# Attention kernel: the causal mask of the diagonal blocks moved from TensorE products to VectorE, and one order of uses for the spare PSUM bank

## The chip, the cores and the metric

The program runs on one NeuronCore of a Trainium2 chip. The metric is the device time of one execution in microseconds (us), as the median of several executions. A core has five engines, each with its own in-order instruction stream: TensorE (PE, with its weight loads shown apart as PEld), VectorE (DVE), ScalarE (ACT), GpSimd (POOL) and SyncE (SP, which here only issues DMAs). They are ordered among each other by semaphores alone. PE writes to eight PSUM banks of 128 partitions by 512 fp32 values.

## The reference

The program computes two transformer-like layers. The change is in the attention of the first one, with 8 batches of 512 tokens, 16 heads of size 8, and two score maps for each head:

```
s1 = jnp.einsum('bhqd,bhkd->bhqk', q1, k1) * scale
s2 = jnp.einsum('bhqd,bhkd->bhqk', q2, k2) * scale
a1 = jax.nn.softmax(jnp.where(causal, s1, neg_inf), axis=-1)
a2 = jax.nn.softmax(jnp.where(causal, s2, neg_inf), axis=-1)
comb = a1 - lam[None, :, None, None] * a2
out = jnp.einsum('bhqk,bhkv->bhqv', comb, v)
```

A layer norm over each head's 16 outputs, a product with `Wo` and a gated residual follow, and then a feed-forward layer, a state-space scan and a mixture of experts, which the change leaves alone.

## The kernel before

**Tiling.** The attention works in rounds, one for each batch (r), and each round in 8 slots (g), one for each group of two heads, so four score maps. The tokens are four blocks of 128. Each map's scores are computed twice. The first time (tile `p1b`, query rows on the partitions, product line L616) serves only to find each row's maximum: DVE reduces a bank over the keys into `bmax` (L853), and at the slot's end all partial maxima into `qneg` (L864). POOL splits the negated maximum into two bf16 parts (`nsp`), PE turns them (`turn_neg`, L731 into the spare bank `auxb`), ACT copies them out (L582) and SP's DMA puts them into the query stack `qs` as extra rows. Two slots later the scores are computed again, transposed and with the maximum already subtracted (tile `p2b`, L668), and ACT takes the exponential into `pT` (L558). POOL zeroes what lies above the diagonal in `pT` (L519). One slot later the products with the values go to `ob` (L682), and one more later the result is copied (`o_sb`, L564), turned (L723) and copied into `oT` (L573).

**Units.** A group's lower triangles are packed into ten banks, called units, handled in five pairs t = 0 to 4: pairs 0 and 2 (units 0, 1, 4, 5) hold the four diagonal blocks of a map each, the others only whole blocks below the diagonal. `p1b` and `p2b` are rings of three banks each, so the first product of a pair waits until DVE has read the first unit of the pair before (semaphore `first_read`, in `bank_free`), and the second product in the same way for ACT's exponential.

**The mask.** Scores above the diagonal must not count in the maximum. Before the four diagonal products of a bank, PE multiplies an identity with the table `causal` (-3e38 above the diagonal, four times side by side, bf16) and lets the scores add onto it: the mask product, L620, four a slot.

**The spare bank.** `auxb` is used in turn for everything else that PE must produce: the turned result, the turned maxima, the transposed input of the next batch (L776, copied to `hT` by ACT at L602), its four projections (`project`, L743; ACT copies the high part at L587, DVE makes the remainder `res` at L858, ACT its middle part at L568, POOL the rest at L540, and SP stores the three parts), its four value products (L770, copied at L598), and for the batch before the turned normalized result (L752) and the product with `Wo` (L763). Each kind has its own pair of semaphores.

**Who does what in a slot.** While a round computes batch r, it prepares batch r+1 (`prep`: transposes in g=0, projections in g=1 to 4, values in g=2 to 5) and finishes batch r-1 (`post`: reciprocals in g=4, POOL's weighted sums in g=4 and 5, DVE's normalization between the units of g=5 and 6, L825 to L839, the output product at the end of g=7, read by DVE at L867). The order is written out by hand in each engine's `slot`. Slot -1 is a prologue that only prepares batch 0.

Of the kernel before, what the change touches and what calls it, by code (L numbers as in the profile page):

```python
# [13 lines left out]
BF16 = mybir.dt.bfloat16  # L14
# [7 lines left out]
P = 128  # L22
# [299 lines left out]
MAPS = 4  # L322
# [10 lines left out]
DIAGONAL, EDGE, MIDDLE = "diagonal", "edge", "middle"  # L333
FIRST = ((DIAGONAL, 0), (EDGE, 0), (DIAGONAL, 1), (EDGE, 1), (MIDDLE, None))
# [14 lines left out]
def lagged(r, g, n):  # L349

    return (r, g - n) if g >= n else (r - 1, g - n + GROUPS)

# [7 lines left out]
def attention(nc, d, k):  # L360
# [3 lines left out]
    with ExitStack() as ctx:  # L364
# [6 lines left out]
        def sem(name):  # L371
# [3 lines left out]
        causal = sb("causal", [P, TILES, P], BF16)  # L375
# [25 lines left out]
        xn_ready, xnT_done, hT_ready, qk_done, hi_ready, res_ready, mid_ready, split_ready, v_done, v_ready = (  # L401
            sem(n) for n in ("xn_ready", "xnT_done", "hT_ready", "qk_done", "hi_ready", "res_ready", "mid_ready",
                             "split_ready", "v_done", "v_ready"))
# [3 lines left out]
        first_unit, first_read, second_unit, exp_done, masked, vs_ready, av_done, o_read, oT_done, oT_read = (  # L407
            sem(n) for n in ("first_unit", "first_read", "second_unit", "exp_done", "masked", "vs_ready", "av_done", "o_read",
                             "oT_done", "oT_read"))
        qneg_ready, nsp_high, nsp_ready, neg_psum, neg_ready = (  # L410
            sem(n) for n in ("qneg_ready", "nsp_high", "nsp_ready", "neg_psum", "neg_ready"))
        rc_ready, og_ready, merged_ready, mT_done, mT_ready, wo_done, gated_ready, post_done = (
            sem(n) for n in ("rc_ready", "og_ready", "merged_ready", "mT_done", "mT_ready", "wo_done", "gated_ready", "post_done"))
# [6 lines left out]
                   oT_done: 2, oT_read: 4, neg_psum: 2, nsp_ready: 2, xnT_done: 1, res_ready: 1, split_ready: 1, v_done: 1, v_ready: 1,  # L420
                   qk_saved[0]: 16, qk_saved[1]: 16, og_ready: 2, merged_ready: 1, mT_done: 1, wo_done: 1, gated_ready: 3, neg_ready: 1, hT_ready: 1}
# [27 lines left out]
        def _(sp):  # L449
# [13 lines left out]
            def slot(r, g, on, prep, post):  # L463
                if on(1):
                    rn, gn = lagged(r, g, 1)
                    sp.wait_ge(neg_ready, rn * GROUPS + gn + 2)
# [78 lines left out]
        def _(act):  # L545
            act.wait_ge(slots_set, 1)

            def slot(r, g, on, prep, post):
# [44 lines left out]
                if prep and 2 <= g < 6:  # L593
                    c, V = g - 2, b * TILES + g - 2
                    act.wait_ge(v_done, V + 2)
                    if c == 0:
                        act.wait_ge(vs_ready, b * GROUPS + 1)
# [10 lines left out]
        def _(pe):  # L608
# [64 lines left out]
            def product(G, a, c):  # L673
# [10 lines left out]
                if c == TILES - 1:  # L684
                    mm.then_inc(av_done, 1)
# [1305 lines left out]
```

## Time and profile before

| | |
|---|---|
| median of 3 runs | 1892.64 us (1891.42 to 1895.62) |
| the profiled execution | 1895.24 us, of it 1893.5 between its first and last instruction |
| busy: PE, DVE, ACT, POOL | 1383.6, 1330.0, 1033.1, 949.4 us |
| attention | about 75 to 835 us of the span |
| mean granted clock of TensorE | 0.839 of full speed |

The busy times are sums over an engine's instructions in the profiled execution. An instruction's row names its line, the tile written and the tiles read, the shape, and, in square brackets, the idle time of its engine ahead of it with what ended that.

### The profile page before, as it was taken

What the parts mean: (1) busy time and instruction counts of PE and PEld (TensorE: products, weight loads), DVE (VectorE), ACT (ScalarE), POOL (GpSimd) and SP (SyncE); (2) the same over time, 40 slices, a digit from 0 to 9 for tenths busy, and PEclk for the clock granted to TensorE, in tenths of its full rate; (3) what the DMA queues carried; (4) which work ended last, traced back from release to release, by engine and by line L of the source; (5) the groups of instructions that cost most, each with busy time, mean ns of one, the idle gap of its engine ahead of it and who ended that gap; (6) DMA issues with size and microseconds to landing.
All of it is one profiled execution on the core that took longest, in us unless ns stands there. A gap on an engine that the chain in (4) does not pass through costs nothing. (4 is left out here: it accounts for less than half of the span.)

```text
span 1893.5 us, 29677 instructions
## 1 busy us (share of the span) xinstructions
PE 1383.6 (73%) x8526; PEld 602.3 (32%) x8589; DVE 1330.0 (70%) x2162; ACT 1033.1 (55%) x1605; POOL 949.4 (50%) x850
## 2 busy tenths in 40 slices
PE   3588888888888888754674465556655788898898
PEld 2133333333333333322342122122212344444343
DVE  3667767676767677836776499999987666566654
ACT  1166666666666566643652444334422677767776
POOL 2032424242424242433882566666772567676677
PEclk7579888888889899876887677777877899999999
DMA  3221313131313131100003354544553766666675
GB/s 96 92 89 48 102 34 100 34 100 34 100 34 100 34 100 39 32 1 0 1 0 92 101 179 162 173 168 165 182 184 115 168 161 170 158 174 170 168 184 137
DMA packets 114314, 197.96 MB, mean 105 GB/s; under 512 B 16300, under 2 KB 49736, under 8 KB 114248
## 3 DMA queue, kind: packets, MB, share of 16 engines
q1 hardware_dynamic: 112808, 195.08, 35.9%
q10 hardware_dynamic: 1440, 2.10, 0.4%
q8 instruction: 30, 0.49, 0.1%
q14 instruction: 36, 0.29, 0.1%
HBM read 167.76 MB, written 28.84 MB: 104 GB/s over the span
## 5 line engine op out<-in xcount | busy, mean ns | idle before, releaser
L853 DVE TENSOR_REDUCE bmax<-p1b 128x4 f32<-128x512 f32 x640 | 414.1, 687 | 183.5 <-PE p1b L616 176.8
L558 ACT ACTIVATE pT<-p2b 128x512 f32<-128x512 f32 x640 | 349.4, 604 | 122.2 <-PE p2b L668 121.1
L1701 POOL TENSOR_TENSOR hid_l<-e_hid,hid_h 128x1024 f16<-128x1024 f32 (+1 forms) x136 | 281.3, 2077 | 134.3 <-ACT hid_h L1843 133.8
L1339 PE MATMUL yb<-ch,ident 128*128 128x512 f32 x256 | 175.8, 825 | 130.3 <-POOL ch L1272 86.9
L1959 DVE TENSOR_TENSOR e_hid<-ub,share 128x1024 f32<-128x1024 f32 x128 | 156.1, 1224 | 152.6 <-ACT ub L1856 131.9
L510 POOL CAST nsp<-qneg 128x16 bf16<-128x16 f32 x64 | 12.7, 198 | 482.7 <-DVE qneg L864 482.7
L682 PE MATMUL ob<-pT,vs 128*32 128x512 f32 (+3 forms) x2048 | 202.4, 482 | 1.3 <-POOL pT L519 1.3
L668 PE MATMUL p2b<-qs,ks 50*128 50x512 bf16 (+3 forms) x1024 | 137.4, 328 | 51.5 <-ACT pT L558 49.8
L1856 ACT ACTIVATE ub<-ub 128x1024 f32<-128x1024 f32 x128 | 129.2, 1009 | 83.3 <-PE ub L1757 81.6
L616 PE MATMUL p1b<-ks,qs 48*128 48x128 bf16 (+2 forms) x1792 | 139.3, 264 | 37.2 <-DVE bmax L853 37.1
L1843 ACT ACTIVATE hid_h<-e_hid 128x1024 f16<-128x1024 f32 (+1 forms) x136 | 139.2, 1024 | 26.8 <-DVE e_hid L1959 26.7
L519 POOL TENSOR_SCALAR_AFFINE_SELECT pT<-pT 128x1280 f32<-128x1280 f32 (+2 forms) x192 | 145.4, 790 | 11.6 <-ACT pT L558 11.6
L1439 ACT ACTIVATE dA<-dt,nA 128x511 f32<-128x511 f32 (+1 forms) x128 | 85.2, 712 | 98.3 <-DVE hs L1529 45.0
L1272 POOL TENSOR_TENSOR ch<-hs,crow 128x1024 f32<-128x1024 f32 x32 | 75.3, 2352 | 119.5 <-DVE hs L1529 93.8
L1339 PEld LDWEIGHTS yb<-ch,ident 128*128 128x128 f32 x256 | 59.8, 253 | 234.8 <-POOL ch L1272 110.1
L1755 PE MATMUL ub<-e_hTh,w_high 128*128 (+1 forms) x256 | 100.9, 394 | 22.2 <-DVE e_hid L1959 22.2
L620 PE MATMUL p1b<-causal,identb 128*128 128x512 bf16 x193 | 91.3, 473 | 35.0 <-DVE bmax L853 22.2
L1529 DVE TENSOR_TENSOR_SCAN hsb<-dA,dBx 128x1024 f32<-128x1024 f32 x32 | 108.8, 3400 | 7.6 <-ACT dA L1439 4.7
L668 PEld LDWEIGHTS p2b<-qs,ks 50*128 50x128 bf16 x1024 | 35.0, 96 | 227.5 <-ACT pT L558 137.7
L1755 PE MATMUL e_yb<-hid_h,w_high 128*128 128x512 f16 x264 | 101.7, 385 | 4.7 <-POOL hid_l L1701 4.0
L1756 PE MATMUL e_yb<-hid_l,w_high 128*128 128x512 f16 x264 | 101.5, 384 | 0.0
L1757 PE MATMUL e_yb<-hid_h,w_low 128*128 128x512 f16 x264 | 101.1, 383 | 0.0
(258 smaller groups left out, 2652.5 us busy)
## 6 DMA issues: line engine op xcount, KB each, us to landing
share<-shares SPq DMA_DIRECT2D x256, 256.0 KB, 4.2
brow<-bc_rows SPq DMA_DIRECT2D x64, 512.0 KB, 4.8
crow<-bc_rows SPq DMA_DIRECT2D x64, 512.0 KB, 4.0
q_stacks<-parts SPq DMA_DIRECT2D x96, 128.0 KB
k_stacks<-parts SPq DMA_DIRECT2D x96, 128.0 KB
qs<-q_stacks SPq DMA_DIRECT2D x128, 96.0 KB, 2.2
ks<-k_stacks SPq DMA_DIRECT2D x128, 96.0 KB, 2.3
qs<-nparts SPq DMA_DIRECT2D x128, 4.0 KB
```

Of the source, the lines that this page charges most:

```text
L519: pool.affine_select(out=block_ap, in_=block_ap, compare_op=ALU.is_ge, fill=0.0, base=0, pattern=[[0, n], [1, P]], channel_multiplier=-1). ...
L558: act.activation(pT[:, g2 % 2, stored(w), :], p2b[bank_of(g2, w)][:, :], ACT.Exp, scale=SCALE).then_inc(exp_done, 1)
L616: return pe.matmul(bank[:, at * P:(at + blocks[1] - blocks[0]) * P], qs[rows, slot, head, c * P:(c + 1) * P], ks[rows, slot, head, blocks[ ...
L668: mm = pe.matmul(p2b[bank_of(g, 2 * t + j)][:, at:at + S - c * P], ks[rows, slot, head, c * P:(c + 1) * P], qs[rows, slot, head, c * P:S], ...
L682: mm = pe.matmul(ob[32 * m:32 * m + 32, c * P:S], vs[:, a, c, m // 2, :], pT[:, a, u, at:at + n], start=(c == 0), stop=(c == TILES - 1), s ...
L853: dve.tensor_reduce(to, bank, AX, ALU.max).then_inc(first_read, 1)
L1339: mm = pe.matmul(yb[:, :], k.ident[:, :], ch[:, m % 4, j, :], start=False, stop=(m == PAIRS - 1 and j == 1), skip_group_check=True)
L1701: pool.tensor_tensor(flat(hid_l[:, place(p), 0:n, :]), flat(hid[:, place(p), 0:n, :]), flat(hid_h[:, place(p), 0:n, :]), ALU.subtract).the ...
L1755: pe.matmul(to, w[0], high, start=start, stop=False, skip_group_check=True)
L1843: act.activation(flat(hid_h[:, place(p), 0:n, :]), flat(hid[:, place(p), 0:n, :]), ACT.Copy).then_inc(hid_rounded, 1)
L1856: act.activation(u, u, ACT.Silu, scale=1.0 / W_SCALE).then_inc(silu_ready, 1)
L1959: dve.tensor_tensor(h, u, flat(share[:, p % SHARES, :, :]), ALU.mult).then_inc(hid_ready, 1)
```

## The change

Three things change. The first is the mask: the mask products go, the first diagonal product of a bank starts the bank itself, and DVE replaces the one reduction of a diagonal bank by four instructions, one for each 128 columns, that add the table `causal` (now one block of 128x128 fp32) to the scores, write the sum to a tile `spare` that nobody reads, and take its maximum into `bmax`. The second is the numbering: all uses of `auxb` get a number in one fixed order (`aux_of`), counted by two semaphores, `aux_done` for PE and `aux_read` for the reader, and every use waits until the use before it is read. The third is a table of places: the value products of a slot come at t=4, for g=3 to 6, ahead of the last products into `ob`; the transposes of `xn` likewise in g=0; `hT` is copied behind ACT's last exponentials of g=0; the middle copy of a projection moves from t=0 to t=1 on ACT; and `res` from ahead of unit 9 to ahead of unit 7 on DVE.

```
+AUX = {"turn_o": 1, "turn_neg": 2, "project": 3, "value": 4, "turn_x": 4, "turn_m0": 3, "turn_m1": 4, "wo": 5}
+AV_AT = (2, 3, 4, 4)
+O_COPY_AT, OT_AT, NEG_COPY_AT, HIGH_AT, MID_AT, HT_AT, V_COPY_AT, MT_AT = 0, 1, 2, 3, 1, 4, 4, (3, 4)
+RES_AT = 6
...
+def aux_of(g):
+
+    kinds = ["turn_o", "turn_neg"]
+    if g == 0:
+        kinds.append("turn_x")
+    if 1 <= g < 5:
+        kinds.append("project")
+    if 3 <= g < 7:
+        kinds.append("value")
+    if g == GROUPS - 1:
+        kinds += ["turn_m0", "turn_m1", "wo"]
+    return sorted(kinds, key=AUX.get)
...
-        causal = sb("causal", [P, TILES, P], BF16)
+        causal = sb("causal", [P, P])
+        spare = sb("spare", [P, MAPS, TILES, P], BF16)
...
-            def mask(bank):
-                pe.matmul(bank[:, :], k.identb[:, :], causal[:, :, :].rearrange("p c t -> p (c t)"), start=True, stop=False, skip_group_check=True)
...
                 if kind == DIAGONAL:
-                    mask(bank[1])
                     for c in range(TILES):
                         for j in range(2):
-                            mm = score(bank[j], c, slot, head, j, c, (c, c + 1), False)
+                            mm = score(bank[j], c, slot, head, j, c, (c, c + 1), c == 0)
...
+                def aux_free(kind):
+
+                    n = aux_use(r, g, kind)
+                    if not isinstance(r, int) or n > 0:
+                        pe.wait_ge(aux_read, n)
...
                         if kind == DIAGONAL:
-                            to = bmax[:, g % 2, 2 * j + head, 8:8 + 3 * BLOCK_STEP + 1:BLOCK_STEP]
+                            dve.sem_inc(passed, 1)
+                            for c in range(TILES):
+                                at_c = 8 + c * BLOCK_STEP
+                                ins = dve.tensor_tensor_reduce(spare[:, u // 4 * 2 + j, c, :], bank[:, c, :], causal[:, :], 1.0, NEG, ALU.add, ALU.max,
+                                                               bmax[:, g % 2, 2 * j + head, at_c:at_c + 1])
+                            ins.then_inc(first_read, 1)
+                            to = None
...
-                    if prep and u == 8 and 1 <= g < 5:
+                    if prep and u == RES_AT and 1 <= g < 5:
```

In the built program, DVE's stream for one plain slot begins before with its first three rows, and continues with the reductions of whole blocks:

```order
L853 TENSOR_REDUCE bmax<-p1b 128x4 x8
L853 TENSOR_REDUCE bmax<-p1b 128x2x2
L858 TENSOR_TENSOR res<-auxb,parts 128x512
L853 TENSOR_REDUCE bmax<-p1b 128x2x2
L864 TENSOR_REDUCE qneg<-bmax 128x16
```

Now one diagonal unit and the rows around it read as follows; an `ISA` row with `bmax 128x1` is the read of the accumulator that the instruction above it left:

```order
L868 ISA spare,bmax<-p1b,causal 128x128
L868 ISA bmax 128x1
L868 ISA spare,bmax<-p1b,causal 128x128
L868 ISA bmax 128x1
L878 TENSOR_REDUCE bmax<-p1b 128x4 x2
```

One reduction has become four pairs of instructions, 32 rows a slot where four stood.

On PE, in a slot with a projection and a value product (g=3) and up to the next slot's first products, before:

```order
L682 MATMUL ob<-pT,vs 32x384 x4
L743 MATMUL auxb<-hT,wqk 128x512
L668 MATMUL p2b<-qs,ks 128x256 x4
L616 MATMUL p1b<-ks,qs 128x256 x4
L682 MATMUL ob<-pT,vs 32x256 x4
L682 MATMUL ob<-pT,vs 32x128 x4
L620 MATMUL p1b<-causal,identb 128x512
L620 MATMUL p1b<-causal,identb 128x512
L616 MATMUL p1b<-ks,qs 128x128 x8
L770 MATMUL auxb<-wv,hT 128x256
```

And in the changed program at the same place (L749 is the projection, L755 the value product, L699 the products into `ob`):

```order
L749 MATMUL auxb<-hT,wqk 128x512
L699 MATMUL ob<-pT,vs 32x384 x4
L684 MATMUL p2b<-qs,ks 128x256 x4
L641 MATMUL p1b<-ks,qs 128x256 x4
L755 MATMUL auxb<-wv,hT 128x256
L699 MATMUL ob<-pT,vs 32x256 x4
L699 MATMUL ob<-pT,vs 32x128 x4
L641 MATMUL p1b<-ks,qs 128x128 x8
```

The masks are gone, and the value product has moved from behind the next slot's first products to ahead of the last products into `ob`; the projection stands one place earlier.

On ACT, the start of slot g=2 before (L558 is the exponential, L564 the copy of `ob`, L568 the middle copy, L573 the copy into `oT`):

```order
L558 ACTIVATE pT<-p2b 128x512
L558 ACTIVATE pT<-p2b 128x512
L564 ACTIVATE o_sb<-ob 128x512
L568 ACTIVATE parts<-res 128x512
L558 ACTIVATE pT<-p2b 128x512
L558 ACTIVATE pT<-p2b 128x512
L573 ACTIVATE oT<-auxb 128x4x68
```

And now (the same kinds at L583, L589, L593 and L599):

```order
L583 ACTIVATE pT<-p2b 128x512
L583 ACTIVATE pT<-p2b 128x512
L589 ACTIVATE o_sb<-ob 128x512
L583 ACTIVATE pT<-p2b 128x512
L583 ACTIVATE pT<-p2b 128x512
L593 ACTIVATE parts<-res 128x512
L599 ACTIVATE oT<-auxb 128x4x68
```

The middle copy has moved behind the second pair of exponentials and stands directly ahead of the copy into `oT`.

## Rows read from the trace of the kernel before

**Rows 1.** the page: busy us of each engine, share of the span, instructions

```profile
PE 1383.6 (73%) x8526; PEld 602.3 (32%) x8589; DVE 1330.0 (70%) x2162; ACT 1033.1 (55%) x1605; POOL 949.4 (50%) x850
```

**Rows 2.** `qneg` instructions: ns min/median/max, first and last start

```profile
L864 DVE TENSOR_REDUCE qneg<-bmax x64: 236/240/246, 84.5 to 812.2; 128x16 f32<-128x80 f32 x64
```

**Rows 3.** windows, slots g=0 to 7: length, busy (instructions), granted clock, DMA share, GB/s

```profile
440.11:455.81 15.70, 12.57 (x109) 5.97 (x111) 9.13 (x18) 7.39 (x14) 3.01 (x6) 0.78 0.08 25
455.81:468.68 12.87, 10.92 (x103) 4.56 (x102) 7.29 (x13) 8.00 (x16) 2.99 (x6) 0.87 0.14 41
468.68:478.38 9.70, 8.52 (x89) 3.62 (x90) 7.10 (x13) 7.33 (x15) 4.12 (x7) 1.00 0.17 48
478.38:488.98 10.60, 9.05 (x93) 3.75 (x92) 7.19 (x12) 7.66 (x16) 4.12 (x7) 1.00 0.37 110
488.98:500.17 11.19, 9.12 (x93) 3.69 (x92) 9.10 (x15) 7.96 (x16) 8.00 (x9) 1.00 0.32 98
500.17:512.85 12.68, 9.10 (x91) 3.74 (x90) 10.17 (x15) 7.16 (x15) 6.45 (x8) 0.92 0.43 133
512.85:526.11 13.26, 11.13 (x92) 4.05 (x94) 11.60 (x26) 7.92 (x16) 2.99 (x6) 0.69 0.23 70
526.11:535.65 9.54, 8.95 (x84) 3.80 (x85) 6.50 (x11) 6.55 (x13) 2.99 (x6) 0.82 0.04 9
sum 95.54, PE 79.36 PEld 33.18 DVE 68.08 ACT 59.96 POOL 34.66; mean PE 9.92 PEld 4.15 DVE 8.51 ACT 7.50 POOL 4.33
```

**Rows 4.** the same for one slot of the last round, without preparation

```profile
748.60:757.15 8.55, 7.19 (x95) 3.10 (x91) 6.70 (x12) 6.58 (x13) 2.99 (x6) 1.00 0.17 51
```

**Rows 5.** waits in 200 to 700 us: total, times, longest

```profile
DVE bmax L853 <- PE p1b L616: 117.4, 121, 2.1
```

**Rows 6.** timeline of that slot: start, duration, engine; [idle before <-releaser]

```profile
751.31 0.38 PE L620 MATMUL p1b<-causal,identb 128*128 128x512 bf16 x1
...
751.62 0.39 PE L668 MATMUL p2b<-qs,ks 50*128 50x512 bf16 x2
...
756.42 0.16 PEld L620 LDWEIGHTS p1b<-causal,identb 128*128 128x128 bf16 x2 [0.20 <-issue]
...
756.97 0.40 PE L616 MATMUL p1b<-ks,qs 48*128 48x128 bf16 x8
```

**Rows 7.** timeline of DVE, three places without waits; below, groups: busy, mean ns

```profile
61.54 5.50 DVE L884 BATCH_NORM_STATS2 bn<-x_tok 128x6 f32<-128x128 f32 x28
...
491.20 2.47 DVE L853 TENSOR_REDUCE bmax<-p1b 128x4 f32<-128x512 f32 x4
...
1708.85 0.08 DVE L1922 MATCH_VALUE_LOAD rest<-top,biased 128x8 f32 x1
1708.92 0.21 DVE L1922 MATCH_REPLACE8 rest<-top,biased 128x64 f32<-128x64 f32 x1
...
L853 DVE TENSOR_REDUCE bmax<-p1b 128x4 f32<-128x512 f32 x640 | 414.1, 687 | 183.5 <-PE p1b L616 176.8
...
L884 DVE BATCH_NORM_STATS2 bn<-x_tok 128x6 f32<-128x128 f32 x64 | 12.7, 276 | 0.5 <-PEq L364 0.5
...
L887 DVE BATCH_NORM_AGGREGATE stats<-bn 128x2 f32<-128x6 f32 x64 | 4.7, 151 | 0.1
...
L867 DVE TENSOR_TENSOR gated<-auxb,gate_a 128x512 f32<-128x512 f32 x8 | 5.5, 692 | 26.0 <-PE auxb L763 26.0
```

**Rows 8.** timeline of all engines, in g=1 and at half clock in g=0

```profile
456.94 0.78 ACT L602 ACTIVATE hT<-auxb,mod 128x512 f32<-128x512 f32 x1 [1.60 <-PE auxb L776]
...
542.04 0.61 PE L616 MATMUL p1b<-ks,qs 48*128 48x384 bf16 x4 [2.23 <-DVE bmax L853]
...
543.48 0.63 PE L620 MATMUL p1b<-causal,identb 128*128 128x512 bf16 x1
```

**Rows 9.** timeline of ACT in g=2, the middle copy of a projection

```profile
470.07 0.64 ACT L568 ACTIVATE parts<-res 128x512 bf16<-128x512 f32 x1
```

**Rows 10.** timeline of POOL in the prologue, the table

```profile
29.75 0.65 POOL L492 TENSOR_SCALAR_AFFINE_SELECT causal<-causal 128x512 bf16<-128x512 bf16 x1
```

More of the change, by code:

```diff
@@ L351, in lagged, with aux_use @@
     return (r, g - n) if g >= n else (r - 1, g - n + GROUPS)
+def aux_of(g):
[9 more added lines that the diff above has]
+    return sorted(kinds, key=AUX.get)
+AUX_PLACE = {use: n for n, use in enumerate((g, kind) for g in range(GROUPS) for kind in aux_of(g))}
+AUX_USES = len(AUX_PLACE)
+def aux_use(r, g, kind):
+    return (r + 1) * AUX_USES + AUX_PLACE[g, kind]
 def stored(w):
@@ new lines, in side @@
+                    if kind == "value":
+                        if not prep:
+                            return skip(kind)
+                        c = g - 3
+                        aux_free(kind)
+                        mm = pe.matmul(auxb[:, 0:H * VD], hT[:, c * P:(c + 1) * P], k.wv[:, :], start=True, stop=True)
+                    if kind in ("turn_m0", "turn_m1"):
+                        if not post:
+                            return skip(kind)
+                        c = int(kind[-1])
@@ new lines, in side @@
+                    mm.then_inc(aux_done, 1)
+                for t in range(PAIRS + 1):
+                    if t == PAIRS:
+                        if g + 1 < GROUPS and on(0) or g + 1 == GROUPS and prep:
+                            rl, gl = (r, g + 1) if g + 1 < GROUPS else (r + 1, 0)
+                            pe.wait_ge(stack_loaded[gl % RING], (use(rl, gl) + 1) * LOADS)
+                            first_pair(rl, gl, 0)
+                    else:
+                        if on(2):
+                            r2, g2 = lagged(r, g, 2)
+                            if t == 0:
+                                pe.wait_ge(neg_loaded[g2 % RING], (use(r2, g2) + 1) * NEG_LOADS)
+                            second_pair(r2, g2, t)
+                        if on(0) and t:
+                            first_pair(r, g, t)
+                    for kind in aux_of(g):
+                        if AUX[kind] == t:
+                            side(kind)
+                    if on(3):
+                        r3, g3 = lagged(r, g, 3)
+                        for n in range(len(CHUNKS)):
+                            if AV_AT[n] == t:
+                                product(r3 * GROUPS + g3, g3 % 2, n)
```

254 lines of the change are left out of this document (105 added, 149 removed).

## Prediction, made before the changed kernel ran

> **What bounds the kernel now.** The page's busy line names no saturated engine: PE 73%, VectorE (DVE) 70% of the span [rows 1]. So I read the windows of one middle round of the attention, cut at the starts of the reduction into `qneg`, which ends each slot on DVE. The 64 slots start their last work between 84.5 and 812.2 us [rows 2], 63 steps of 11.55 us on average. One round takes 95.54 us, with PE busy 79.36, DVE 68.08, ACT 59.96 [rows 3]. No engine is full; the slots are of two kinds. In g=1 to 3 and 7 PE sets the pace: PE has 8.5 to 10.9 us of work and DVE idles 2.6 to 5.6 us of the slot. In g=4 to 6 DVE does the normalization of the last batch between its bank reductions and has 9.1 to 11.6 us of work in 11.2 to 13.3 us. A slot without preparation, of the last round, takes 8.55 us with PE at 7.19 and DVE at 6.70 [rows 4]. The whole change therefore moves work from PE to DVE where the two are 10% apart: PE leads in most slots, and after the change DVE will.
>
> What holds PE in such a slot is its ring with ACT (the second product of a pair waits for the exponential of the pair before) and its ring with DVE (three banks): in 500 us of the middle rounds DVE waits for first products 117.4 us in 121 places [rows 5], which is most of its idle time.
>
> **What the change removes, on PE.** Four mask products a slot, 32 a round. From the starts in one slot the first costs 0.31 us (751.31 to 751.62), the second as much, the two ahead of the next slot 0.55 (their weight load at 756.42 to the product behind them at 756.97) [rows 6]: 1.17 us a slot at full clock. Walking the 8.55 us slot without them, all else as it stands, PE's own path would be 7.4 us.
>
> **What it adds, on DVE.** Four of ten reductions a slot go; each becomes four times a 128-column add-and-maximum from PSUM and a read of the accumulator, 16 pairs a slot. Neither operation is in the trace. Nearest rows for the cadence when nothing is waited for: 28 statistics of 128 columns took 5.50 us, so (5.50-0.276)/27 = 0.193 us from start to start, 128 columns at 1.04 ns and 0.060 fixed; four reductions of 512 columns from PSUM took 2.47 us, (2.47-0.687)/3 = 0.594, again 0.061 fixed; and a tiny instruction that loads state for the next one (8 columns) holds its successor for 0.07 us [rows 7]. A pair is then 0.193 + 0.062 = 0.255. Bounds: below, nothing can beat the 128 columns plus one fixed part, 0.193. Above, if each of the two ran alone to its end, the duration of the statistics, 0.276, plus that of a 12-column aggregate, 0.151: 0.427 [rows 7]. I take 0.256, because the loader pair is the nearest kind (two instructions that share engine state) and it isn't held. That the second operand is an fp32 table shouldn't matter: the product of a PSUM bank with an fp32 gate takes 0.692 for 512 columns, as the reduction does (0.687) [rows 7].
>
> The Trainium skill speaks to this twice. "VectorE: DVE Perf Modes", section on two Vector instructions with no wait between them, says that an operation with accumulator output is two instructions, each judged on its own, and held only when start quadrants change; here all start at partition 0. It would give the 0.256 that I take. "Vector Engine (DVE) Microarchitecture Reference", section 5.2, puts the fixed part at about 75 ns; an estimate by it is a pair of 0.284 and a sum of about 1899 us, no gain. The rows here (60 and 61 ns) are below its figure.
>
> So DVE's own work in a plain slot is 16 x 0.256 + 6 x 0.594 + 0.3 (`qneg`, and the gap to the first unit) + 4 x 0.05 (a wait at each unit) = 8.2 us, against PE's 7.4. Break-even with the 8.55 of now is a pair of 0.278.
>
> **The walk through the rings.** Unit 0 of a diagonal pair now frees its bank after 1.1 us instead of 0.69, so PE's next first product starts 0.4 later. But it has then unit 1 (another 1.05) for 0.43 us of product and latency, so DVE doesn't starve. That is why I let DVE run nearly without gaps in plain slots.
>
> **The numbered spare bank and the moved copies.** These edits change waits. (1) The copy into `hT` and the transposes of `xn` come before the next slot's first exponentials. Now ACT waits 1.60 us for the transposes and copies for 0.78 before it can start them [rows 8], and PE's next first product and DVE stand behind those: with DVE in the lead, this goes from g=1. (2) The subtraction `res` moves from ahead of unit 9 to ahead of unit 7. It needs ACT's high copy of the projection, which comes some 0.75 us later than DVE gets there: a new DVE stall of 0.75 in g=1 to 3. (3) The middle copy moves on ACT from before the exponentials of t=1 to behind them, ahead of the copy into `oT`, 0.64 long [rows 9]. PE's `turn_neg` waits for `oT`; with its masks gone PE arrives about 0.6 earlier than now, so it stands there: about 0.3 of g=2 and 3 reaches DVE. Behind it in PE's queue are the products into `ob`, which nobody needs soon. (4) The value product now stands ahead of the last products into `ob` and of the next slot's first product, and waits for `res`; 0.1 more in g=3. Where DVE has its own extra work (g=4 to 6) these are hidden.
>
> Slot by slot, now and after (us):
> g=0: 15.70, 14.0 (1.0 less of waiting for the output product, since the two masks in front of it go and DVE arrives 0.5 later; 1.1 for two masks at half clock; 0.4 more until the first bank is free)
> g=1: 12.87, 9.8 (8.2 + 0.6 `res` + 0.75 stall + 0.2; item 1)
> g=2: 9.70, 10.0
> g=3: 10.60, 10.1
> g=4: 11.19, 11.7 (8.2 + 2.0 reciprocal and gate + 0.6 + 0.9)
> g=5: 12.68, 12.8 (8.2 + 3.7 of three 1024-column steps, + 0.9 until POOL's sum is there)
> g=6: 13.26, 14.0 (8.2 + 5.8)
> g=7: 9.54, 9.3 (PE: 7.4 + two sets of transposes, partly at half clock)
> Sum 95.5 to 91.7.
>
> The granted clock takes some of it back. It stands at 1.00 in g=2 to 4 and at 0.69 in g=6, where PE waits for DVE [rows 3]; behind a wait of 2.23 us for DVE a mask product takes 0.63 instead of 0.38 us [rows 6, 8], the lower of the two levels, 1.2 GHz for 2.4. With DVE in the lead PE waits more. I add 0.8: a round of 92.5, so 3.0 saved.
>
> Sum: six middle rounds x 3.0 = 18; the first 2.5, the last 1; the prologue 1.5, of it some 0.8 for a table a quarter as wide, which POOL clears and fills (the fill alone 0.65 now [rows 10]), which DVE waits for at the start. Together 23. The profiled execution took 1895.24, the median of the runs is 2.6 lower: 1895.2 - 23 - 2.6 = 1870 us.
>
> **Rivals.** What a measurement can tell from no change is about 0.2%, 4 us.
> *The read of the accumulator waits for the sum* (slower; it ends on the other side). Then the pair is 0.276 + 0.062 = 0.338, 0.082 more; x 16 x 64 = 84 us more, 1954. For: it reads what the instruction before it makes. Against: the loader pair isn't held. From 0.28 on it decides. Fully serial, 0.427, it would be 175 more, 2045.
> *A larger fixed part.* The accumulating form may start 0.014 us later each than the instructions of [rows 7] do; with 28 ns more in a pair, 1024 pairs cost 29 us, 1899. For: these two instructions are in no row. Against: three kinds of instruction there agree within 0.01. (This is the second page's case.)
> *The clock.* PE at half clock needs some 12 us for a plain slot (7.4 by 0.63/0.38, [rows 6, 8]), more than DVE's 8.2. If g=1, 2, 3 and 7 spend half their time so, each gains 1.5: +6 a round, 1918. For: PE's busy share falls from 0.84 [rows 4] to about 0.7 in plain slots. Against: while PE is slow it is busy all the time, and in g=2 and 3 it keeps the projection and 80% share.
> *The new stalls eat the gain*: items 2 to 4 at twice my size, 3 a round, 24 us: 1889 to 1895, no change. For: they stand in four slots of eight; against: each was walked from rows.
>
> **How the numbers follow.** My forecast 0.52 (1845 to 1888); pair held, partly or fully, 0.18 (of it 0.10 above 1958); larger fixed part 0.06; clock 0.14; stalls eat it 0.10. Faster: 0.50 of the first, 0.04 of the last two, 0.54; same 0.07; slower 0.39. The range leaves out 0.10 above and some 0.06 below: 1848 to 1958.
>
> **What would show it.** The durations and starts of the four add-and-maximum instructions of a unit: 1.0 us from first to fifth start if I am right, 1.35 or 1.7 if held. The `qneg` starts 92 to 93 us apart from round to round; DVE busy over 80 of them, PE under 72. The wait of DVE for the high copy where `res` stands, and ACT's 1.60 us wait for the transposes gone. A granted clock in g=2 and 3 clearly under 1 would make the clock rival right. I'd be wrong above all through the pair: 0.01 us in it is 10 us of the kernel.

## The result and the profile after

The changed kernel took 1898.89 us (median of 7 runs, 1897.21 to 1902.93), the kernel before, on the same chip, 1892.28 us (7 runs, 1883.02 to 1895.62). The ratio is 1.0043, 95% interval 1.0023 to 1.0063: slower, by about 0.4%, where 1870 us and faster was forecast. The time lies inside the stated range (1848 to 1958), on the wrong side of the kernel before. A few executions of the kernel before, of e9 and of e14 further down ran far slower at a lower clock; the ratios leave them out, and e14's trace isn't read, since its profiled execution was one of them.

The busy line of the page, beside [rows 1], and VectorE's two new kinds of row (count, total us, mean ns, idle before them):

```profile
PE 1359.2 (72%) x8333; PEld 592.1 (31%) x8333; DVE 1389.7 (73%) x3954; ACT 1031.5 (54%) x1605; POOL 950.2 (50%) x850
...
L868 DVE CUSTOM_DVE_ANT_0 spare<-p1b,causal 128x128 bf16<-128x128 f32 x1024 | 228.0, 286 | 30.2 <-PE p1b L641 21.2 <-DVE vsum L849 1.9 <-DVE msum L843 1.9
L868 DVE DVE_READ_ACCUMULATOR2_ANT bmax<- 128x1 f32 x1024 | 84.5, 83 | 0.0
```

Work moved from PE to DVE as intended. The windows between the starts of `qneg` in a middle round, g=0 to 7 (it is the round behind that of [rows 3]; the second to sixth middle rounds are alike within 0.2 us, in either kernel):

```profile
540.48:557.63 17.15, 11.27 (x109) 5.85 (x108) 10.07 (x45) 7.23 (x15) 3.00 (x6) 0.80 0.08 24
557.63:568.98 11.35, 9.75 (x100) 3.73 (x96) 8.17 (x40) 7.28 (x15) 2.98 (x6) 0.85 0.16 46
568.98:579.65 10.67, 9.05 (x88) 3.39 (x86) 8.17 (x41) 7.50 (x15) 4.12 (x7) 0.84 0.19 57
579.65:590.25 10.60, 9.47 (x90) 3.82 (x88) 8.16 (x40) 7.88 (x16) 4.12 (x7) 0.84 0.37 110
590.25:602.89 12.64, 9.82 (x92) 3.79 (x88) 10.02 (x42) 8.04 (x16) 7.98 (x9) 0.86 0.32 95
602.89:616.02 13.13, 8.87 (x92) 3.57 (x90) 11.24 (x42) 8.13 (x17) 6.44 (x8) 0.87 0.39 119
616.02:629.66 13.64, 10.39 (x88) 3.86 (x86) 12.45 (x54) 6.99 (x15) 2.99 (x6) 0.63 0.21 61
629.66:639.49 9.83, 8.54 (x82) 3.63 (x78) 7.67 (x39) 6.97 (x14) 2.99 (x6) 0.83 0.04 11
sum 99.01, PE 77.15 PEld 31.64 DVE 75.95 ACT 60.02 POOL 34.62; mean PE 9.64 PEld 3.96 DVE 9.49 ACT 7.50 POOL 4.33
```

The round takes 99.01 us for 95.54. Three of eight slots are clearly longer: g=0 by 1.5, g=2 by 1.0 and g=4 by 1.5; g=1 gained 1.5. The granted clock in g=2 to 4, at 1.00 before, is 0.84 to 0.86. PE is busy longer in g=3 than before (9.47 for 9.05) although four products went. In a slot without preparation, of the last round, the gain is there, 7.67 us for the 8.55 of [rows 4]:

```profile
759.05:766.72 7.67, 6.57 (x86) 2.79 (x84) 7.47 (x40) 6.38 (x13) 2.99 (x6) 1.00 0.18 55
```

DVE's timeline at the start of a round, with PE's next product, and DVE's waits from 200 to 700 us (total, times, longest):

```profile
547.38 1.15 DVE L920 TENSOR_SCALAR xn<-x_tok,stats,rstd 128x128 f32 x4 [2.77 <-issue]
548.48 0.29 DVE L868 CUSTOM_DVE_ANT_0 spare<-p1b,causal 128x128 bf16<-128x128 f32 x1
548.69 0.08 DVE L868 DVE_READ_ACCUMULATOR2_ANT bmax<- 128x1 f32 x1
548.69 0.29 DVE L868 CUSTOM_DVE_ANT_0 spare<-p1b,causal 128x128 bf16<-128x128 f32 x1
...
549.47 0.61 PE L641 MATMUL p1b<-ks,qs 48*128 48x384 bf16 x4 [5.19 <-DVE bmax L868]
```

```profile
DVE res L883 <- ACT parts L613: 23.6, 21, 1.2
DVE xn L920 <- issue: 13.2, 5, 2.8
```

A pair of instructions costs 0.21 us (548.48 to 548.69). But DVE now stands for 2.77 us ahead of the first instruction of a round, waiting for nothing that the profile shows, five times; the five are the five jumps back of the loop over the middle rounds. PE waits 5.19 us behind it. DVE also waits about 1.1 us at each `res`.

### The profile page after: what moved, and what is told of

Same layout as the page of the kernel before. It is cut to its first block and busy times, and to the rows that moved or that the text cites. A ratio compares the mean times of both kernels' runs of the same rounds, so it can differ in the third digit from the quotient of the medians.

```text
span 1897.1 us, 31496 instructions
## 1 busy us (share of the span) xinstructions
PE 1359.2 (72%) x8333; PEld 592.1 (31%) x8333; DVE 1389.7 (73%) x3954; ACT 1031.5 (54%) x1605; POOL 950.2 (50%) x850
## 5 line engine op out<-in xcount | busy, mean ns | idle before, releaser
L583 ACT ACTIVATE pT<-p2b 128x512 f32<-128x512 f32 x640 | 349.9, 605 | 189.9 <-PE p2b L684 189.1
L878 DVE TENSOR_REDUCE bmax<-p1b 128x4 f32<-128x512 f32 x384 | 248.2, 685 | 56.9 <-PE p1b L641 52.4
L1364 PE MATMUL yb<-ch,ident 128*128 128x512 f32 x256 | 180.8, 845 | 125.9 <-POOL ch L1297 87.5
L868 DVE CUSTOM_DVE_ANT_0 spare<-p1b,causal 128x128 bf16<-128x128 f32 x1024 | 228.0, 286 | 30.2 <-PE p1b L641 21.2
L699 PE MATMUL ob<-pT,vs 128*32 128x512 f32 (+3 forms) x2048 | 231.6, 543 | 2.0 <-POOL pT L544 1.3
L641 PE MATMUL p1b<-ks,qs 48*128 48x128 bf16 (+2 forms) x1792 | 147.0, 274 | 116.1 <-DVE bmax L868 70.0
L684 PE MATMUL p2b<-qs,ks 50*128 50x512 bf16 (+3 forms) x1024 | 142.9, 340 | 45.7 <-ACT pT L583 45.2
L544 POOL TENSOR_SCALAR_AFFINE_SELECT pT<-pT 128x1280 f32<-128x1280 f32 (+2 forms) x192 | 145.3, 790 | 10.1 <-ACT pT L583 10.1
L641 PEld LDWEIGHTS p1b<-ks,qs 48*128 48x128 bf16 x1792 | 69.8, 106 | 182.4 <-DVE bmax L868 90.0
```

The costliest lines, as they stand in the source:

```text
L544: pool.affine_select(out=block_ap, in_=block_ap, compare_op=ALU.is_ge, fill=0.0, base=0, pattern=[[0, n], [1, P]], channel_multiplier=-1). ...
L583: act.activation(pT[:, g2 % 2, stored(w), :], p2b[bank_of(g2, w)][:, :], ACT.Exp, scale=SCALE).then_inc(exp_done, 1)
L641: return pe.matmul(bank[:, at * P:(at + blocks[1] - blocks[0]) * P], qs[rows, slot, head, c * P:(c + 1) * P], ks[rows, slot, head, blocks[ ...
L684: mm = pe.matmul(p2b[bank_of(g, 2 * t + j)][:, at:at + S - c * P], ks[rows, slot, head, c * P:(c + 1) * P], qs[rows, slot, head, c * P:S], ...
L699: mm = pe.matmul(ob[32 * m:32 * m + 32, q0:q1], vs[:, a, c, m // 2, :], pT[:, a, u, at:at + q1 - q0], start=(n == 0), stop=(n == len(CHUNK ...
L868: ins = dve.tensor_tensor_reduce(spare[:, u // 4 * 2 + j, c, :], bank[:, c, :], causal[:, :], 1.0, NEG, ALU.add, ALU.max, bmax[:, g % 2, 2 ...
```

## Experiments

All figures in one place first. "Last" is the start of the last `qneg` in the profiled execution, where the attention's maxima end. After it the programs took another 1073 to 1087 us, whatever the mask, so it tells more about the attention than the total does. The attention lost 11.4 us by it, more than the total did; what follows the attention differs by up to 13 us between the profiled executions. Kernels of different groups ran on different chips; the ratio is to the kernel before on the same chip.

| kernel | median us | ratio, 95% interval | last, us |
|---|---|---|---|
| before | 1892.28 | 1 | 812.2 |
| changed | 1898.89 | 1.0043, 1.0023 to 1.0063 | 823.6 |
| e1 mask alone | 1907.47 | 1.0102, 1.0064 to 1.0140 | 823.1 |
| e2 numbering and places alone | 1875.09 | 0.9909, 0.9878 to 0.9941 | 792.9 |
| e3 changed, rounds written out | 1881.37 | 0.9949, 0.9926 to 0.9971 | 797.1 |
| e4 before, rounds written out | 1866.89 | 0.9879, 0.9852 to 0.9905 | 788.6 |
| e5 changed, loop shifted | 1889.36 | 1.0008, 0.9984 to 1.0032 | 810.8 |
| e6 changed, idle mask products | 1916.47 | 1.0146, 1.0112 to 1.0181 | 840.9 |
| e7 half the masks on DVE | 1895.15 | 1.0027, 1.0006 to 1.0048 | 812.1 |
| e8 e2, rounds written out | 1864.90 | 0.9870, 0.9836 to 0.9905 | 785.6 |
| e9 e2, longer DVE loop | 1889.17 | 0.9983, 0.9967 to 0.9999 | 812.1 |
| e10 e2, transposes of `xn` later | 1873.53 | 0.9913, 0.9880 to 0.9945 | 806.5 |
| e11 changed, `res` later | 1884.94 | 0.9971, 0.9953 to 0.9990 | 807.4 |
| e12 e8, masks on DVE at the ends | 1866.47 | 0.9864, 0.9834 to 0.9895 | 778.0 |
| e13 changed, written out, `res` later | 1859.83 | 0.9841, 0.9809 to 0.9873 | 773.1 |
| e14 e13, half the masks on PE | 1889.29 | 0.9954, 0.9923 to 0.9985 | not read |
| e15 e8, `res` later | 1864.25 | 0.9840, 0.9816 to 0.9865 | 782.6 |
| e16 e15, some masks on DVE | 1878.41 | 0.9937, 0.9915 to 0.9960 | 793.5 |

### Which part of the change lost

**e1** is the kernel before with the mask of the change alone; **e2** the changed kernel with its numbering and places, and the mask products and single reductions of before:

```
e2, against the changed kernel:
+                    mask(bank[1])
-                            mm = score(bank[j], c, slot, head, j, c, (c, c + 1), c == 0)
+                            mm = score(bank[j], c, slot, head, j, c, (c, c + 1), False)
...
+                            to = bmax[:, g % 2, 2 * j + head, 8:8 + 3 * BLOCK_STEP + 1:BLOCK_STEP]
```

> The kernel before with only the mask moved to VectorE (the sixteen add-and-maximum pairs a slot; DVE's loop over the middle rounds grows as in the changed kernel); numbering and places of the kernel before. Theory 'fetch' (the loss is the 2.8 us wait of DVE at the loop's back edge, which comes from the longer loop, and PE's half clock behind it): the wait is here too, and the time is 1890 to 1903, near the changed kernel. Theory 'places' (the early remainder, the late middle copy and the moved products lose it): no 1.2 us waits of the remainder for ACT's high copy, and the time is 1870 to 1885. If both hold, half and half: about 1885 with the back-edge wait in the rows. Theory 'clock' (DVE leads, PE idles and falls to half clock whatever the order): 1890 to 1905, clocks under 0.9 in g=1 to 4 without the wait being the reason.

> The changed kernel's numbering and places, with the mask products and single reductions of the kernel before. Theory 'places': slower than the kernel before by 8 to 25 us (1900 to 1917), with a wait of the remainder for ACT's high copy of up to 1 us in g=1 to 4. Theory 'fetch': DVE's loop is short again, no wait at the back edge, and the time is within 6 us of the kernel before (1886 to 1898), faster if the earlier hT copy counts.

Both missed their forecasts: e1 is slower than any theory had it, e2 faster. The parts pull in opposite ways. The numbering with its places gains 0.9%, the mask by itself loses 1.0%; between e2 and the changed kernel lie 1.3%. "Places" is refuted as the cause by itself: the stall that I had forecast at `res` stands in e2 (DVE waits for the high copy 21 times there too) and e2 is the faster one. e1 has the wait at the jump back (13.1 us in five).

### The wait at the jump back

In **e3**, **e4** and **e8** the middle rounds of the changed kernel, of the one before and of e2 are written out:

```
-            with eng.Fori(1, B - 1) as r:
+            for r in range(1, B - 1):
```

> The changed kernel with its six middle rounds written out one after the other on every engine, in place of the hardware loop: the same instructions in the same order, no branch back. Theory 'fetch': the 2.77 us wait ahead of the first normalization instruction of each round goes, PE's 5 us wait behind it shrinks, and the kernel is 15 to 30 us faster than the changed one: 1870 to 1884. Theory 'places' or 'clock': the slots g=0 and g=1 hardly change, 1892 to 1900. Instruction loading itself costs something everywhere: 1900 or more, with waits for nothing in the middle of rounds.

> The kernel before with its middle rounds written out in the same way: what the unrolling does by itself. No DVE wait at the back edge stands in its trace, so by theory 'fetch' it stays within 4 us of the kernel before (1888 to 1896); if unrolling helps or hurts by itself it does so here as well, and the difference to the run before it is what the changed kernel's longer loop costs.

> Numbering and places of the change, masks on PE (as in the second experiment), middle rounds written out on every engine. The second experiment showed PE waiting 2.6 us for no other engine at its own back edge. Unrolled it should lose that: six rounds of 2.3 to 3.9 us, 1852 to 1862. If the gain of unrolling in the kernel before (23 us) came from something else, for example from a lucky order of the clock, this one stays at 1870 to 1878.

The wait is gone from e3, with 17 us by the medians. But writing out also gained 10 us over e2 (e8) and 23 over the kernel before (e4, against its forecast), and in neither e2 nor the kernel before does DVE have such a wait. In e2 it is PE that waits, at the same jump; the second row is e2's branch on PE's sequencer, the third the same branch in the kernel before (ns min/median/max of six passes, of which the last doesn't jump):

```profile
PE p2b L692 <- issue: 11.3, 5, 2.6
```

```profile
L467 PEldq COMPARE_BRANCH  x6: 82/3807/4244, 245.8 to 710.0; - x6
```

```profile
L443 PEldq COMPARE_BRANCH  x6: 76/208/239, 249.8 to 727.7; - x6
```

So an engine waits at the jump for itself. PE's wait stands in e2, e6, e9 and e10, and neither in the kernel before nor in the changed one, although the loops of e2 and of the kernel before hardly differ on PE (891 and 886 instructions in the trace beside the products); why is open. In the kernel before no engine waits: on each the next instruction starts within 0.4 us of the branch. What e4 gained, 3.4 us a round, lies in g=0 and g=1, 15.70 and 12.87 us at clocks of 0.78 and 0.87 in [rows 3]:

```profile
427.55:441.48 13.93, 11.50 (x113) 5.68 (x113) 9.01 (x18) 7.37 (x14) 2.98 (x6) 0.88 0.11 30
441.48:452.66 11.18, 9.54 (x104) 3.97 (x98) 7.29 (x12) 7.78 (x16) 2.98 (x6) 1.00 0.17 49
```

DVE's normalization `xn` starts there 4.1 us after the slot's start, for 4.6 with the loop. That this half microsecond is what raised the clock is not shown. So e3 alone doesn't tell how much of its 17 us is the wait. In the changed kernel DVE's wait of 2.77 us comes on top of PE's path (it starts after DVE has read the output product, which PE makes early in the slot). Written out, the changed kernel is still 16 us slower than e2 written out (e3 against e8, on different chips; 0.8% by the ratios).

**e5** shifts the loop in DVE's stream, **e9** lengthens DVE's loop in e2 by 100 instructions that lie in waits, **e7** puts only units 0 and 1 on DVE. The counts in the texts below (244, 344, 356, 468) leave out some register and semaphore instructions: between two jumps of DVE the trace holds 248 in the kernel before, 250 in e2, 355 in e9, 378 in e7 and 505 in the changed kernel.

```
e5:
+            for i in range(80):
+                dve.memset(pad[:, i:i + 1], 0.0)
             dve.wait_ge(slots_set, SET)
e9:
+                    lengthen(60, 100)
                     dve.wait_ge(aux_done, aux_use(r, g, "wo") + 1)
...
+                        lengthen(15 * j, 15 * j + 15)
                         dve.wait_ge(hi_ready, J + 1)
e7, DVE:
+                        if kind == DIAGONAL and u >= 4:
+                            to = bmax[:, g % 2, 2 * j + head, 8:8 + 3 * BLOCK_STEP + 1:BLOCK_STEP]
```

> The changed kernel with 80 one-column memsets added to VectorE's stream in the prologue, inside its 9.2 us wait for POOL's tables, so that they cost nothing by themselves; all they do is shift where the loop's 468 instructions lie in the stream: from 451 to 919 in the changed kernel to 531 to 999 here. Theory 'where the loop lies' (instructions are held in aligned blocks of 256, two at a time; the loop of the changed kernel touches three, that of the kernel before, 227 to 469, two, and this one two again): the 2.77 us wait ahead of the first normalization instruction of each middle round is gone, g=0 goes from 17.1 to about 14.3, the kernel 12 to 20 us faster than the changed one: 1879 to 1887. Theory 'loop length' (it is the 468 instructions themselves or the branch, wherever they lie): nothing changes, 1896 to 1901, and the wait stays.

> The second experiment's kernel (numbering and places of the change, masks on PE) with 100 one-column memsets a round added on VectorE where it waits for others anyway: 40 ahead of its wait for the output product, 15 ahead of each wait for ACT's high copy. One took 28 ns in the padded kernel, so 2.8 us a round, all of it inside waits. DVE's loop grows from 244 to 344 instructions, and its work otherwise stays. Theory 'loop length': a wait of 2.5 to 3.4 us for nothing appears ahead of the first normalization instruction of each middle round, as in the half-mask kernel with its 356, and g=0 grows by up to 2.8 us where PE's own wait at the back edge doesn't cover it: 1878 to 1892 against 1875. Theory 'kind of instruction' (the accumulating instructions or their second form cause the wait, not their number): no such wait, 1872 to 1879.

> Half of the change's mask: units 0 and 1 are masked on VectorE as in the changed kernel, units 4 and 5 by mask products on PE as before; numbering and places are the changed kernel's. DVE's loop has 356 instructions, at 339 to 695, in two aligned blocks of 256. Theory 'where the loop lies': no 2.8 us wait of DVE at the back edge. Each mask moved costs DVE 0.25 us and saves PE 0.29; with half of them PE keeps 0.6 us more work a slot than in the changed kernel. If wait and clock are what the change lost, this is faster than both the kernel before and the changed one: 1868 to 1880. If moving any mask costs in proportion, it lies half way between the masks on PE (1875) and the changed kernel (1899): 1887.

DVE's waits at the loop's first instruction, e5, e9 and e7:

```profile
DVE xn L923 <- issue: 16.4, 5, 3.4
```

```profile
DVE xn L933 <- issue: 13.0, 5, 2.7
```

```profile
DVE xn L940 <- issue: 13.2, 5, 2.7
```

e9 settles that it isn't the kind of instruction: no mask is on DVE, g=1 to 3 are as long as in e2, and the wait is there, with 14 us of time (g=0 takes 17.8 to 18.5 us for 13.3 to 16.7). In e5, 80 instructions further on, the wait is longer, not gone. But this doesn't refute "where the loop lies": a loop of 505 instructions fits into two blocks of 256 at 8 of 256 places alone, so the shift could hardly have done what that theory asked of it. Length and place aren't told apart by these runs. e5's time fell between its two forecasts, and not for a shorter wait: g=1 ran at 1.00 in every middle round, 9.8 us for 11.35.

```profile
451.60:461.38 9.78, 8.09 (x99) 3.41 (x96) 8.18 (x41) 7.28 (x15) 2.98 (x6) 1.00 0.20 54
```

The Trainium skill's page "Runtime: NRT & Kernel Launch", section "Instruction fetch mechanics", has a rule of this kind: a jump back to code outside the two blocks of 256 instructions that are held makes the engine wait for a fetch. The waits agree with it in kind. That its two blocks give the border seen no run shows: 248 and 250 instructions went without a wait, 355, 378 and 505 did not, and where a block begins in the stream no trace tells.

### PE's clock

**e6** is the changed kernel with PE's old mask products on top, over a table of zeros:

```
+                pe.matmul(bank[:, :], k.identb[:, :], flat[:, :, :].rearrange("p c t -> p (c t)"), start=True, stop=False, skip_group_check=True)
```

> The changed kernel, its masks on VectorE, but PE also does the four mask products a slot of the kernel before, with a table of zeros, so that they change no value: PE has its old work, DVE its new. Theory 'clock' (without the mask products PE's share of work falls, its clock drops to 0.84 to 0.87 in g=1 to 4, and that is what makes these slots 10.6 to 11.4 us long): the clock goes back to 1.00 in g=1 to 3, the slots come to 10.9, 10.1, 10.2 and 12.0, and the kernel is 5 to 12 us faster than the changed one although it does more: 1887 to 1894. Theory 'DVE sets the pace' (the slots are long for the sum of DVE's own work and its waits): the same 1896 to 1901. Theory 'PE sets the pace': slower by up to 1.2 us a slot in the plain slots and g=1 to 3, 1910 to 1930.

Windows of g=1 to 3, of e6 and then of e2:

```profile
471.53:482.26 10.73, 9.56 (x105) 3.73 (x102) 8.08 (x40) 7.42 (x15) 2.98 (x6) 1.00 0.16 51
482.26:492.22 9.96, 8.72 (x98) 3.44 (x92) 8.08 (x40) 7.50 (x15) 4.12 (x7) 1.00 0.17 46
492.22:502.26 10.04, 8.80 (x90) 3.40 (x84) 8.09 (x40) 7.88 (x16) 4.14 (x7) 1.00 0.40 119
```

```profile
445.14:455.87 10.73, 9.39 (x104) 3.74 (x102) 7.29 (x13) 7.41 (x15) 2.98 (x6) 1.00 0.18 49
455.87:465.83 9.96, 8.66 (x98) 3.48 (x92) 7.23 (x13) 7.49 (x15) 4.12 (x7) 1.00 0.16 45
465.83:475.87 10.04, 8.74 (x90) 3.44 (x84) 7.23 (x12) 7.87 (x16) 4.14 (x7) 1.00 0.40 118
```

With more to do PE ran g=1 to 3 at 1.00, and these slots came out 0.6 to 0.7 us shorter than in the changed kernel, to the hundredth those of e2: DVE's 0.8 us of extra work is hidden there. The clock theory holds for them, but not for the whole: g=0 grew to 18.7 us and g=4 stayed at 0.87, so that e6 is the slowest of all. In g=0 of e6 PE has also a wait at the jump, which it doesn't have in the changed kernel; how much of the growth that is isn't shown:

```profile
PE p2b L695 <- issue: 11.8, 5, 2.7
```

The plain comparison is within one kernel. In e3 the same slot g=1 of two rounds:

```profile
445.24:454.56 9.32, 7.55 (x88) 3.13 (x86) 8.13 (x41) 6.97 (x14) 2.99 (x6) 1.00 0.18 49
```

```profile
537.83:549.08 11.25, 9.40 (x96) 3.77 (x92) 8.18 (x41) 7.10 (x15) 2.99 (x6) 0.85 0.14 40
```

The same slot of the program, 1.9 us apart, a little of it because eight products fell on the other side of its edge. At 0.85 part of the slot ran at 1.2 GHz. e13, below, has the pair with equal counts.

### The places

**e10** is e2 with `"turn_x": 5`, **e11** the changed kernel with `RES_AT = 8`, **e15** that change in e8.

> The second experiment's kernel with one number changed: the transposes of the next input stand behind the first products of g=1 on PE, as in the kernel before, instead of ahead of them. If the prediction's first item is what the numbering gained (12.9 to 10.7 us in g=1), g=0 and g=1 together give back 1 to 2.2 us a round, 7 to 14 us: 1882 to 1889. If the gain of g=1 came from the clock or from the rest of the table, within 3 us of 1875.

> The changed kernel with the remainder ahead of unit 9 again in place of unit 7. In the changed kernel DVE waits 1.0 to 1.2 us there for ACT's high copy in g=1 to 4. Theory 'that stall is paid' (prediction's item 2): the wait goes, and each of the four slots loses 0.5 to 1.0 us: 12 to 24 us faster, 1875 to 1887. Theory 'the slots follow PE at its lower clock': DVE waits the same time for PE's products elsewhere, the slots stay within 0.3 us, and the kernel within 5 us of 1899; a slot changes only where its clock does.

> e8 (rounds written out, numbering and places of the change, masks on PE) with the remainder ahead of unit 9 again. DVE waits 1.0 us for the high copy in g=1 to 4 in e8, but PE leads there: nothing should come of it, 1862 to 1868. If the wait is paid even where PE leads, 0.3 to 0.5 us in three slots of six rounds: 1855 to 1860.

e10's time is e2's, as its second forecast had it: in the medians the earlier transposes are worth nothing that shows. In the trace g=1 takes 11.33 us at full clock in one round for 10.73 in e2, and 12.8 to 12.9 at 0.87 in most others: at equal clock the slot is 0.6 us longer. The profiled execution took 1883.55 us, 10 above the kernel's median, so its windows stand for an unlucky case.

e11 is 0.7% faster than the changed kernel, as its first forecast had it: the wait for the high copy was paid, where DVE leads. Its g=2 in two successive rounds shows which way:

```profile
462.70:473.32 10.62, 9.07 (x86) 3.49 (x86) 8.17 (x40) 7.68 (x17) 4.10 (x7) 0.84 0.21 61
```

```profile
557.32:566.74 9.42, 7.80 (x86) 3.09 (x86) 8.18 (x40) 7.49 (x17) 4.11 (x7) 1.00 0.18 52
```

At 0.84 nothing changed (10.62 for 10.67). The gain is in slots that now reach 1.00, g=1 and 2 in three of the six middle rounds (g=3 in two of them) and g=4 in the other three; at 1.00 the wait itself is worth 0.2 (e5 had 9.64 there in one round, `res` early). In e15, where PE leads, g=2 and 3 are 0.35 us shorter each, g=4 and 5 are 0.5 and 0.6 longer, and the time is e8's, as forecast.

### Masks where they pay

**e12** is e8 with the masks on DVE in the first round and in g=1 to 3 of the last. **e13** is the changed kernel with both of DVE's waits removed (rounds written out, `RES_AT = 8`), **e14** the same with units 4 and 5 masked on PE. **e16** is e15 with masks on DVE as in e12 and, in the middle rounds, in pair 0 of g=1 to 4 and 7:

```
+def on_vector(r, g, t):
+
+    return r == 0 or r == B - 1 and 1 <= g < 4 or t == 0 and (r < B - 1) and g in (1, 2, 3, 4, 7)
```

> The unrolled kernel with masks on PE (e8), and masks on VectorE only in the first round and in the slots g=1 to 3 of the last, where DVE has no normalization and PE leads. The traces so far give 3.5 us for the first round (69.3 against 72.8 us for its slots g=1 to 7) and 2.5 us for three slots of 7.67 against 8.49: 6 us off the 1864.9, 1857 to 1861, and the attention's last maximum at about 780 us against 785.6. If what the masks cost on VectorE were in the instructions themselves and not in the place, this one would be slower than e8.

> The changed kernel with its middle rounds written out and the remainder ahead of unit 9 again: neither the back-edge wait nor the wait for the high copy is left on DVE. At full clock its slots would be 14.0, 9.8, 9.4, 9.4, 11.2, 13.1, 13.6 and 8.2 (from earlier runs), 88.7 a round, 2.6 under the 91.3 of masks on PE. Theory 'clock': only some of the slots reach 1.00, each of the others is 1.0 to 1.5 us longer, so the rounds differ from one another by such steps with the same DVE work, and the kernel comes to 1866 to 1878, no faster than with masks on PE (1865). Theory 'DVE's own work and waits' (with those two waits gone the rest follows from the sum): 1845 to 1858 and equal rounds of 89.

> As the run before it, but units 4 and 5 are masked by PE's products (half the masks on each engine). Theory 'clock': PE has 0.6 us more work a slot, more of the slots reach a clock of 1.00 (10.2, 9.6, 9.7, 11.4 in g=1 to 4), and it is as fast or faster than with all masks on VectorE: 1858 to 1870. Theory 'DVE's own work': half way between all masks on DVE and all on PE in every slot at the same clock.

> Rounds written out, the remainder ahead of unit 9. Masks all on VectorE in the first round and in g=1 to 3 of the last; in the middle rounds units 0 and 1 of the slots g=1 to 4 and 7 on VectorE, the rest on PE, so that DVE's long slots g=5, 6 and 0 keep their single reductions. From the slots seen at full clock: 0.4 us less each in g=1 to 3, 6 rounds, 7 us, and 6 us for the first and last round, against 1865: 1850 to 1860. If the clock falls in one of these slots a round, the 7 us are gone again: 1858 to 1866.

e12 did in the attention what was forecast (778.0 for 785.6), but its median is e8's, on another chip: the total doesn't show it. e14 and e16 missed, as did e7: each is slower than both of its forecasts. e14's executions fall into two groups, 1873 to 1876 and 1889 to 1894 us. In e16 g=0 takes 15.3 to 15.6 us in every middle round but the first and g=7 9.9 to 10.1, where e15 has 12.6 to 15.4 and 8.2 to 8.8; the clock in g=7 is 0.83 for e15's 1.00. Why mixed masks do worse there isn't settled.

e13 fell between its two forecasts. It has the lowest median, and its ratio is that of e15. Its rounds aren't equal, as "DVE's own work" would have them: they differ in steps with the clock. Its middle round with the highest clock, g=0 to 7, and then g=2 and g=3 of the round before:

```profile
510.42:523.92 13.50, 10.63 (x110) 5.92 (x112) 10.07 (x46) 7.20 (x14) 2.98 (x6) 0.87 0.11 32
523.92:533.68 9.76, 7.87 (x96) 3.32 (x92) 8.17 (x40) 7.55 (x16) 2.98 (x6) 1.00 0.18 52
533.68:542.92 9.24, 7.66 (x86) 3.09 (x86) 8.04 (x40) 7.49 (x16) 4.11 (x7) 1.00 0.21 61
542.92:552.15 9.23, 6.91 (x65) 2.69 (x65) 8.14 (x40) 7.03 (x15) 4.11 (x7) 1.00 0.42 130
552.15:563.33 11.18, 8.25 (x93) 3.35 (x92) 10.00 (x42) 7.87 (x16) 7.99 (x9) 1.00 0.31 92
563.33:576.24 12.91, 8.91 (x117) 3.88 (x116) 11.16 (x43) 8.78 (x19) 6.42 (x8) 1.00 0.41 130
576.24:589.67 13.43, 9.61 (x86) 3.79 (x86) 12.45 (x54) 6.95 (x15) 2.98 (x6) 0.75 0.23 70
589.67:599.04 9.37, 8.16 (x80) 3.53 (x78) 7.54 (x40) 6.64 (x14) 2.98 (x6) 0.82 0.05 13
```

```profile
441.56:452.39 10.83, 9.25 (x86) 3.46 (x86) 8.13 (x41) 7.49 (x16) 4.10 (x7) 0.84 0.24 75
452.39:463.13 10.74, 8.42 (x66) 3.13 (x66) 8.13 (x40) 7.16 (x15) 4.10 (x7) 0.84 0.34 104
```

The same instructions take 9.24 and 9.23 us at 1.00, 10.83 and 10.74 at 0.84, and PE's busy time for the same products grows by what the slot grows: 7.66 to 9.25 in g=2, 6.91 to 8.42 in g=3. Four of e13's six middle rounds are of the first kind in these slots. With its two waits gone the changed kernel gains 2.0%, and the mask on DVE is then level with masks on PE under the same conditions (e15); that it pays is not shown.

## Why the prediction was wrong

**The step that failed** is the sum over the slots, 95.5 to 91.7 and 92.5 with the clock. Against the 99.0 measured, slot by slot: g=0 3.1 us more than I had, g=1 1.6, g=2 0.7, g=3 0.5, g=4 0.9, g=5 0.3, g=7 0.5, g=6 0.4 less. Two things were missing or too small in it. e9 shows the first by itself, e3 with what else writing out does; e11 and e13 show the second.

*A wait that no term had.* In g=0 DVE stands 2.77 us at the jump back, after its loop went from 248 to 505 instructions. I counted what the 32 new rows a slot take to run, not what a longer loop does at its jump. 14.0 + 2.8 is 16.8 of the 17.15.

*"I add 0.8" for the clock* was mis-sized. The rival had it better: 1.5 us for a slot that spends half its time at 1.2 GHz, and "a granted clock in g=2 and 3 clearly under 1 would make the clock rival right". It is 0.84, and such a slot costs 1.5 to 1.6 us over its twin at 1.00 (e13). The rival's round, 92.5 and 6, is near the 99.0 measured. Its total, 1918, wasn't reached: it charged the 6 us in eight rounds, and the first and the last lost nothing (69.25 and 85.14 us for 72.80 and 85.41). It didn't name g=4, where the clock fell too.

**The pair** was put at 0.256 us and measured 0.21; the bounds (0.193 and 0.427) held it, and both the rival of the held read and the one of the larger fixed part are refuted. The plain slot came to 7.67 for my 8.2, DVE's busy time in a round to 75.95, under the 80 that I had named as the sign; PE's, named as under 72, to 77.15, its products being slower at the lower clock. So the term that I called decisive was wrong in the kernel's favour, and it still lost. That the prediction names the 1899 us that were measured, in its estimate with a fixed part of 75 ns and in the rival of the larger fixed part, is luck: both come to it through a pair of 0.284. (The break-even pair that it gives as 0.278 is 0.280 by its own sum.)

**The places.** (1) The copy into `hT` first: right in g=1, ACT's long wait went, 0.6 us at equal clock, though e10's total doesn't show it. (2) The `res` stall was forecast as 0.75 in g=1 to 3 and measured 1.0 to 1.2 in g=1 to 4; removing it gave 14 us (e11), most of it through the clock, which is half of the 29 us between forecast and result. Items (3) and (4) weren't taken apart. What I hadn't seen is that the numbering and its places together are a gain of 0.9% (e2), 19 us of attention, with g=7 at 8.33 for 9.54 and a clock of 1.00. "The new stalls eat the gain" is refuted for the stalls by themselves, since e2 has them; with DVE in the lead the one at `res` costs what e11 shows.

**The prologue and the first round** gained more than forecast: the first `qneg` starts at 80.9 for 84.5, and the first round is 3.5 us shorter. The prologue's gain isn't shown to be the smaller table's: e2, with the old table, starts at 81.1, e8 with the same prologue at 84.2, and e1, with the small one, at 84.4. The last round gained only 0.3, though its plain slots gained 0.9 each: g=4 to 7 of it gave that back.

**Slot by slot at full clock** my numbers were near or too high: 9.8, 10.0, 10.1, 11.7, 12.8 for g=1 to 5, against 9.76, 9.24, 9.23, 11.18, 12.91 in e13.

**What stays open**: what decides whether a given slot of a round gets the full clock (e13's rounds differ with the same instructions), whether the length of the loop or its place makes the jump back cost, and from where on, why PE waits there in e2 and not in the kernel before, what raised the clock in e4, and why mixed masks are worse than either pure form with the rounds written out (e14, e16; in the loop e7 lies between e2 and the changed kernel, close to the changed one).

## What to carry to other kernels

When an edit multiplies the instructions of an engine inside a hardware loop, look at the loop's length before the durations: here 100 tiny instructions, free in themselves, cost 14 us through a wait of 2.7 us at each jump back (e9), which only a row "waits for nothing" at the loop's first instruction betrays. And run the control: writing the loop out gained even more in the kernel before, which had no such wait (e4), so that gain alone proves nothing about the wait. When work is taken off TensorE so that another engine leads, price each slot at both clock levels; the saving per product is small beside a fallen clock. And split a change that has several parts: here one part gained 0.9% and the other lost 1.3%.

## What the hardware showed that I had not expected

The accumulating instruction starts its successor 0.21 us later although its own row says 0.29 and the read of the accumulator 0.08: the rows overlap. One-column memsets ran 28 ns from start to start (80 in 2.28 us in e5), half of the 0.06 us fixed part that I had worked out. At a jump back PE's branch took 0.21 us in one kernel and 3.8 in another (the kernel before and e2). And writing six rounds out, with no other edit, made the kernel before 1.2% faster (e4), though none of its engines waited at the jump.
